# A hand-ordered transformer block on five engines: another order of all steps, with weight loads, a modulation product and weight splits moved

## The reference

```python
ada = silu(c) @ W_ada + b_ada                      # [32, 6*288]
shift_msa, scale_msa, gate_msa, shift_mlp, scale_mlp, gate_mlp = split(ada, 6)
h = layernorm(x) * (1 + scale_msa) + shift_msa
qkv = h @ W_qkv + b_qkv                            # 288 -> 864
attn = softmax(q k^T / sqrt(18))                   # 16 heads, 256 x 256
x = x + gate_msa * ((attn @ v) @ W_proj + b_proj)
h = layernorm(x) * (1 + scale_mlp) + shift_mlp
x = x + gate_mlp * (gelu(h @ W_fc1 + b_fc1) @ W_fc2 + b_fc2)   # 288 -> 1152 -> 288
```

## Time and profile before

| | |
|---|---|
| Time, median of 3 runs | 1203.75 us (1203.28 to 1208.13) |
| The profiled execution's own time | 1203.89 us |
| Its span, first to last instruction | 1202.1 us |
| Mean granted TensorE clock, share of full speed | 0.984 |
| PE busy | 1158.4 us (96%), 10375 matmuls |
| DVE busy | 920.6 us (77%) |
| ACT busy | 858.0 us (71%) |
| POOL busy | 579.2 us (48%) |
| HEAD of TensorE | first step at 14.8 us |

### The profile page before, as it was taken

The page is one execution under the profiler, slowest core; times in us unless marked ns, Lnnn a source line. Parts: engine busy times, 40 slices in busy tenths (PEclk is TensorE's granted clock), DMA queues, the critical chain, the costliest instruction groups (busy, mean ns, idle before and its releaser), DMA issues.

```text
span 1202.1 us, 28774 instructions
## 1 busy us (share of the span) xinstructions
PE 1158.4 (96%) x10375; PEld 993.9 (83%) x10375; DVE 920.6 (77%) x1928; ACT 858.0 (71%) x1485; POOL 579.2 (48%) x619
## 2 busy tenths in 40 slices
PE   6888999999999999999999999999999999999987
PEld 5666788888888888888888888888888888888777
DVE  5578878878878788887778888877888887877553
ACT  4378777777777777777777787777777777778721
POOL 3012444555544445554454555445455544544664
PEclk9779999999999999999999999999999999999999
DMA  9454554455555445555544555555445555444220
GB/s 276 137 172 156 163 164 147 150 175 168 164 159 163 149 148 173 166 171 164 163 151 151 159 179 165 165 159 167 143 149 181 164 165 161 158 148 156 83 68 20
DMA packets 133814, 186.93 MB, mean 156 GB/s; under 512 B 24284, under 2 KB 102150, under 8 KB 133675
## 3 DMA queue, kind: packets, MB, share of 16 engines
q1 hardware_dynamic: 133513, 184.66, 48.9%
q10 hardware_dynamic: 162, 0.44, 0.1%
HBM read 119.92 MB, written 64.60 MB: 153 GB/s over the span
## 4 chain that ended last, share of the span: by engine, by line
PE 92%; DVE 3%; ACT 2%; DMA 1%; issue 1%; SPq 0%; POOL 0%; ACTq 0%; POOLq 0%; DVEq 0%
PE a_bank L855 13%; PE x_bank L768 12%; PE turn_bank L822 10%; PE b_bank L855 9%; PE score_bank L793 7%; PE st_bank L810 7%; PE b_bank L869 7%; PE b_bank L870 6%; PE b_bank L871 6%; PE a_bank L836 5%; PE x_bank L776 5%; PE x_bank L742 2%; PE a_bank L742 1%; ACT e L942 1%; PE x_bank L745 1%
## 5 line engine op out<-in xcount | busy, mean ns | idle before, releaser
L1128 DVE TENSOR_REDUCE mx<-score_bank 128x2 f32<-128x512 f32 x512 | 332.3, 685 | 94.6 <-PE score_bank L793 92.8
L942 ACT ACTIVATE e<-st_bank 128x1024 f32<-128x1024 f32 x256 | 262.3, 1024 | 163.9 <-PE st_bank L810 163.3
L1285 POOL TENSOR_TENSOR gl<-gl_raw,gh 128x512 fp32r<-128x512 f32 (+1 forms) x160 | 197.2, 1241 | 180.8 <-DVE gh L1193 180.8
L935 ACT CAST ql<-mxt 4x256 fp32r<-4x256 f32 x512 | 205.7, 402 | 5.3
L869 PE MATMUL b_bank<-w,gh 128*128 128x288 f32 x576 | 179.1, 311 | 2.0 <-DVE tmp L1199 1.9
L870 PE MATMUL b_bank<-w,gh 128*128 128x288 f32 x576 | 170.6, 296 | 0.0
L871 PE MATMUL b_bank<-w,gl 128*128 128x288 f32 x576 | 169.6, 295 | 0.0
L822 PE MATMUL turn_bank<-e,ve 128*32 128x256 f32 x2048 | 125.8, 387 | 0.1
L810 PE MATMUL st_bank<-ql,kl 58*128 58x256 f32 x1024 | 117.9, 309 | 6.1 <-ACT e L942 5.0
L793 PE MATMUL score_bank<-kl,ql 58*128 58x256 f32 x1024 | 120.7, 314 | 2.7 <-DVE mx L1128 1.9
L855 PE MATMUL a_bank<-xh,w 128*128 128x256 f32 x640 | 112.2, 298 | 5.5 <-DVE xr L1107 4.0
(11 more groups left out here) (152 smaller groups left out, 2490.9 us busy)
## 6 DMA issues: line engine op xcount, KB each, us to landing
qk_rows<-qst SPq DMA_DIRECT2D x128, 256.0 KB, 3.7
ql<-qk_rows SPq DMA_DIRECT2D x384, 72.0 KB
kl<-qk_rows SPq DMA_DIRECT2D x378, 72.0 KB
o_rows<-on SPq DMA_DIRECT2D x128, 128.0 KB
gate<-gates SPq DMA_DIRECT2D x32, 432.0 KB, 4.5
xin<-in_x SPq DMA_DIRECT2D x32, 288.0 KB, 4.1
x<-in_x SPq DMA_DIRECT2D x32, 288.0 KB, 4.0
out<-x SPq DMA_DIRECT2D x32, 288.0 KB, 2.2
```

The lines of the kernel that those rows point to most:

```text
L935: last = nc.scalar.copy(rows[:, :, :, a, :], src)
L942: nc.scalar.activation(e[:, j % 4, :, :, :].rearrange("p i u l -> p (i u l)"), st_bank[:, :, :, :].rearrange("p i u l -> p (i u l)"), ACT. ...
L1128: nc.vector.tensor_reduce(mx[:, j // HP, i, :, col:col + 1], score_bank[i][:, :].rearrange("p (t l) -> p t l", t=NT), AX.X, ALU.max).then_ ...
L1285: nc.gpsimd.tensor_tensor(gl[:, cols], g[:, cols], gh[:, cols].bitcast(F32), ALU.subtract).then_inc(g_lo, 1)
```

## The change

All fifteen tables are replaced by others; the steps in them are the same, save for what follows.

- **TensorE's period.** In the old ORDER the 16 steps of 58 rows (`s`, `st`) stand as seven pairs and two single steps; one `pv` stands alone between `fc2` and `qk`, one behind a single `s`. In the new one they stand as eight pairs; one `pv` is behind a pair, one in front of a pair. Three pairs are followed by a turning (before: four), and one turning (`("xt", 2, 1)`) stands between `fc1` steps.
- **Scores by head.** For sequences 0 and 1 the step `s` is replaced by two steps `sh`, one for each head: 2 matmuls, both in the same half of the array.
- **Second modulation in pieces.** `mod` becomes ten steps of 3 products each, spread over the start of HEAD.
- **Weight loads.** Loads 7 to 11 leave the block ahead of SyncE's HEAD and become steps `load`, the first behind `("qkr", 0, 5)`.
- **Splits.** Of the nine weight splits in HEAD, the two of the packed 32 channels (5 and 8) stay on VectorE, the other seven (3, 4, 6, 7, 9, 10, 11) go to GpSimd, with a semaphore of their own, `w_late`.

The diff, with the other tables and the rest of the HEAD lists left out:

```diff
 PE_ORDER = [
-    ("fc2", -3, 0), ("proj", -2, 0), ("st", 0, 1), ("s", 0, 6), ("xt", 2, 0), ("proj", -2, 1), ("st", 0, 2),
-    ("s", 0, 7), ("xt", 2, 1), ("fc2", -3, 1), ("st", 0, 3), ("fc2", -3, 2), ("pv", 0, 0), ("qk", 2, 0),
-    ("fc2", -3, 3), ("s", 1, 0), ("st", 0, 4), ("lt", -2, 0), ("fc2", -3, 4), ("s", 1, 1), ("st", 0, 5),
-    ("lt", -2, 1), ("qk", 2, 1), ("fc2", -3, 5), ("s", 1, 2), ("st", 0, 6), ("fc1", -2, 0), ("s", 1, 3),
-    ("st", 0, 7), ("qk", 2, 2), ("fc1", -2, 1), ("s", 1, 4), ("pv", 0, 1), ("fc1", -2, 2), ("v", 2, 0),
-    ("fc1", -2, 3), ("st", 1, 0), ("s", 1, 5), ("fc1", -2, 4), ("v", 2, 1),
+    ("st", 0, 2), ("s", 0, 7), ("fc1", -3, 2), ("xt", 2, 1), ("fc1", -3, 3), ("fc1", -3, 4), ("qk", 2, 0),
+    ("fc2", -3, 0), ("proj", -2, 0), ("s", 1, 0), ("st", 0, 3), ("proj", -2, 1), ("fc2", -3, 1), ("qk", 2, 1),
+    ("s", 1, 1), ("st", 0, 4), ("pv", 0, 0), ("fc2", -3, 2), ("st", 0, 5), ("s", 1, 2), ("lt", -2, 0), ("qk", 2, 2),
+    ("fc2", -3, 3), ("st", 0, 6), ("s", 1, 3), ("lt", -2, 1), ("fc2", -3, 4), ("st", 0, 7), ("s", 1, 4), ("v", 2, 0),
+    ("fc2", -3, 5), ("pv", 0, 1), ("s", 1, 5), ("st", 1, 0), ("v", 2, 1), ("fc1", -2, 0), ("st", 1, 1), ("s", 1, 6),
+    ("xt", 3, 0), ("fc1", -2, 1),
 ]
...
 PE_HEAD = [
+    ("xt", 0, 0), ("xt", 0, 1), ("qk", 0, 0), ("qk", 0, 1), ("qk", 0, 2), ("gate2", 0, 0), ("gate5", 0, 0),
+    ("v", 0, 0), ("gate5", 0, 1), ("v", 0, 1), ("mod", 0, 0), ("gate5", 0, 2), ("xt", 1, 0), ("gate2", 0, 1),
+    ("mod", 0, 1), ("xt", 1, 1), ("mod", 0, 2), ("mod", 0, 3), ("sh", 0, 0), ("sh", 0, 1), ("gate2", 0, 2),
+    ("sh", 0, 2), ("sh", 0, 3), ("qk", 1, 0), ("sh", 0, 4), ("sh", 0, 5), ("mod", 0, 4), ("sh", 0, 6), ("sh", 0, 7),
+    ("qk", 1, 1), ("sh", 0, 8), ("sh", 0, 9), ("mod", 0, 5), ("mod", 0, 6), ("mod", 0, 7), ("mod", 0, 8),
+    ("mod", 0, 9), ("qk", 1, 2), ("sh", 0, 10), ("st", 0, 0), ("sh", 0, 11), ("v", 1, 0), ("sh", 0, 12),
+    ("st", 0, 1), ("sh", 0, 13), ("v", 1, 1), ("st", 0, 2), ("sh", 0, 14), ("xt", 2, 0), ("sh", 0, 15), ("st", 0, 3),
+    ("xt", 2, 1), ("pv", 0, 0), ("qk", 2, 0), ("sh", 1, 0), ("st", 0, 4), ("sh", 1, 1), ("sh", 1, 2), ("st", 0, 5),
...
 ACT_HEAD = [
+    ("xt", 0, 0), ("xt", 0, 1), ("round", 0, 0), ("round", 0, 1), ("qk", 0, 0), ("qk", 0, 1), ("qk", 0, 2),
+    ("v", 0, 0), ("qkr", 0, 0), ("round", 0, 2), ("qkr", 0, 1), ("qkr", 0, 2), ("v", 0, 1), ("qkr", 0, 3),
+    ("qkr", 0, 4), ("qkr", 0, 5), ("xt", 1, 0), ("xt", 1, 1), ("round", 0, 3), ("round", 0, 4), ("qk", 1, 0),
+    ("round", 0, 5), ("qk", 1, 1), ("mb", 0, 0), ("qk", 1, 2), ("st", 0, 0), ("v", 1, 0), ("st", 0, 1), ("v", 1, 1),
+    ("st", 0, 2), ("xt", 2, 0), ("st", 0, 3), ("xt", 2, 1), ("mb", 0, 1), ("qk", 2, 0), ("st", 0, 4),
...
 DVE_HEAD = [
+    ("qk", 0, 1), ("qk", 0, 2), ("ln1_stats", 1, 0), ("ln1_apply", 1, 0), ("ln1_apply", 1, 1), ("xt", 1, 0),
+    ("ln1_stats", 2, 0), ("xt", 1, 1), ("max", 0, 0), ("max", 0, 1), ("split", 0, 5), ("gates", 0, 0),
+    ("ln1_apply", 2, 0), ("max", 0, 2), ("max", 0, 3), ("max", 0, 4), ("max", 0, 5), ("qk", 1, 0), ("max", 0, 6),
+    ("split", 0, 8), ("max", 0, 7), ("mt", 0, 0), ("qk", 1, 1), ("ln1_apply", 2, 1), ("max", 0, 8), ("mod", 0, 0),
+    ("max", 0, 9), ("max", 0, 10), ("qk", 1, 2), ("max", 0, 11), ("ln1_stats", 3, 0), ("max", 0, 12), ("max", 0, 13),
...
 POOL_HEAD = [
+    ("clr", 0, 0), ("ln1_stats", 0, 0), ("clr", 0, 1), ("xt", 0, 0), ("clr", 1, 0), ("split", 0, 3),
+    ("ln1_stats", 1, 0), ("split", 0, 4), ("ln1_stats", 2, 0), ("xt", 1, 0), ("split", 0, 6), ("clr", 1, 1),
+    ("split", 0, 7), ("clr", 2, 0), ("xt", 2, 0), ("ln1_stats", 3, 0), ("clr", 2, 1), ("xt", 3, 0),
+    ("ln1_stats", 4, 0), ("clr", 3, 0), ("clr", 3, 1), ("ol", 0, 0), ("xt", 4, 0), ("proj", 0, 0), ("proj", 0, 1),
...
 SYNC_HEAD = [
+    ("qkr", 0, 5), ("load", 0, 7), ("qkr", 0, 12), ("qkr", 0, 13), ("qkr", 0, 14), ("qkr", 0, 15), ("qkr", 0, 16),
+    ("load", 0, 8), ("qkr", 0, 17), ("qkr", 0, 18), ("qkr", 0, 19), ("qkr", 0, 20), ("ln1_stats", 3, 0),
+    ("qkr", 0, 21), ("load", 0, 9), ("qkr", 0, 22), ("qkr", 0, 23), ("qkw", 1, 0), ("load", 0, 10), ("qkw", 1, 1),
+    ("qkw", 1, 2), ("res", 0, 0), ("qkr", 1, 0), ("qkr", 1, 1), ("qkr", 1, 2), ("qkw", 1, 3), ("qkw", 1, 4),
+    ("qkr", 1, 3), ("qkr", 1, 4), ("qkr", 1, 5), ("qkr", 1, 6), ("qkr", 1, 7), ("qkr", 1, 8), ("qkr", 1, 9),
+    ("qkr", 1, 10), ("qkr", 1, 11), ("qkr", 1, 12), ("ln1_stats", 4, 0), ("qkr", 1, 13), ("qkr", 1, 14),
+    ("qkr", 1, 15), ("qkr", 1, 16), ("qkr", 1, 17), ("qkr", 1, 18), ("qkr", 1, 19), ("qkr", 1, 20), ("qkr", 1, 21),
...
         minus_set = sem("minus_set")
         minus_rows = sem("minus_rows")
         w_split = sem("w_split")
+        w_late = sem("w_late")
         c_loaded = sem("c_loaded")
         ada_first = sem("ada_first")
         choice = sem("choice")
@@ -467,7 +471,7 @@
                            for v in (w2_raw[:, 1, f:f + 3, :], w2[:, 0, f:f + 3, :], w2[:, 1, f:f + 3, :]))
             loads.append(("fc2", w_fc2, None, raw, hi, lo, 3 * C, f))
         I_PROJ = 5
-        N_FIRST = 3
+        N_FIRST, N_EARLY = 3, 7
         w_loaded = sems("w_loaded", len(loads))
 
 
@@ -684,9 +688,9 @@
             sp.wait_ge(minus_set, 1)
             for r0, nr in ((O_REM[2][0], O_REM[2][2]), (O_REM[3][0], O_REM[3][2] + 1)):
                 sp.dma_start(minus_p[r0:r0 + nr, 0:1], minus_p[r0:r0 + nr, 1:2]).then_inc(minus_rows, 16)
-            for i in range(N_FIRST, len(loads)):
+            for i in range(N_FIRST, N_EARLY):
                 load_weights(i)
-            run(SYNC_HEAD, SYNC_ORDER, SYNC_TAIL, {"ln1_stats": ln1_stats, "res": res, "qkw": qkw, "qkr": qkr, "ow": ow,
+            run(SYNC_HEAD, SYNC_ORDER, SYNC_TAIL, {"load": lambda _b, i: load_weights(i), "ln1_stats": ln1_stats, "res": res, "qkw": qkw, "qkr": qkr, "ow": ow,
                              "sr": sum_read, "sw": rc_write, "rr": rc_read, "or": o_read, "store": store})
             for i in range(2):
                 sp.wait_ge(stored[i], 16 * (B // 2))
@@ -702,23 +706,31 @@
             last.then_inc(ada_turned, 1)
 
             pe.wait_ge(ada_sT, 1)
+            def mod_piece(n, i, c, r):
+
+                c0 = MOD_OF[2 * n + i] * C
+                cols = slice(c0 + c * P, min(c0 + (c + 1) * P, c0 + C))
+                for k, (_r, nr) in enumerate(K_ROWS):
+                    rows = nr + (k == 2)
+                    to = mod_of[n][:, i, c, :] if c < 2 else mod_of[n][REM * r:REM * (r + 1), i, c, :]
+                    last = nc.tensor.matmul(to, w_ada_sb[k][0:rows, cols], sT[0:rows, k, :],
+                                            start=(k == 0), stop=(k == 2))
+                return last
+
+            MOD_PIECES = [(i, c, r) for i in range(2) for c in range(3) for r in range(1 if c < 2 else 3)]
+
             def mod_columns(n):
 
-                for i in range(2):
-                    c0 = MOD_OF[2 * n + i] * C
-                    for c in range(3):
-                        for k, (_r, nr) in enumerate(K_ROWS):
-                            rows = nr + (k == 2)
-                            for r in range(1 if c < 2 else 3):
-                                to = mod_of[n][:, i, c, :] if c < 2 else mod_of[n][REM * r:REM * (r + 1), i, c, :]
-                                cols = slice(c0 + c * P, min(c0 + (c + 1) * P, c0 + C))
-                                last = nc.tensor.matmul(to, w_ada_sb[k][0:rows, cols], sT[0:rows, k, :],
-                                                        start=(k == 0), stop=(k == 2))
+                for i, c, r in MOD_PIECES:
+                    last = mod_piece(n, i, c, r)
                 last.then_inc(ada_mod, 1)
 
-            def second_mod(_b, _n):
-                pe.wait_ge(ada_rest, 16 * 3)
-                mod_columns(1)
+            def second_mod(_b, n):
+                if n == 0:
+                    pe.wait_ge(ada_rest, 16 * 3)
+                last = mod_piece(1, *MOD_PIECES[n])
+                if n == len(MOD_PIECES) - 1:
+                    last.then_inc(ada_mod, 1)
 
             def gate_rows(v, k):
                 if k == 0:
@@ -796,6 +808,23 @@
                         if t == NT - 1:
                             last.then_inc(s_full[i], 1)
 
+            def s_head(b, h):
+                j, i = h // 2, h % 2
+                slot, use = half_use(b, j // HP)
+                if j % HP == 0:
+                    pe.wait_ge(qk_rows[slot], 16 * READS * (use + 1))
+                if b == 0 and h == 0:
+                    pe.wait_ge(consts, FIRST_SET)
+                    pe.wait_ge(kl_chosen, SLOTS)
+                    pe.wait_ge(ql_cleared, 1)
+                wait(pe, s_max[i], PAIRS * b + j)
+                rows = slice(TILE * i, TILE * i + KM)
+                for t in range(NT):
+                    last = nc.tensor.matmul(score_bank[i][:, t * L:(t + 1) * L],
+                                            ql[rows, slot, j % HP, t * P:(t + 1) * P], kl[rows, slot, j % HP, :],
```

(25 more changed lines are left out.)

136 lines of the change are left out of this document (60 added, 76 removed), and 148 rows, old and new, of tables (ACT_HEAD, ACT_ORDER, ACT_TAIL, DVE_TAIL).

## The result

The change makes the kernel slower: 1258.32 us (median of 4 runs, 1256.40 to 1260.13) against 1203.93, ratio 1.0442 [1.0417, 1.0468]. The forecast was 1184, the range 1175 to 1198. By span, 1258.0 against 1202.1 us, the loss of 55.9 us is made up as follows. TensorE's steps were matched one by one between the two traces, and a length is read from the first matmul of a step to the first of another.

What follows compares the result with a forecast made beforehand. TensorE, never idle between about 140 and 1085 us, was taken to bound the kernel. 1203.9 less 14.6 for the periods and 5 for the first `st`, the rest at 0, gave 1184 us, range 1175 to 1198.

Steps and rivals of the forecast that it cites:

- The edges of TensorE's period: Repeated order: pairing score steps and two fewer groups between products save 0.54 us a period, 14.6 us over 27 periods.
- Whether the others keep up: Repeated order: no new wait, with slacks of 0.2 us at `st` 5's exponential and 0.4 at the casts before `st` (1,0).
- The rule that was weighed: Splits in HEAD: GpSimd shares its way to SBUF with VectorE, so up to 14.6 us of DVE work could stretch, once.
- The rival of the other side: Repeated order: DVE late with a half's last maxima behind a POOL-stretched subtraction, 1.0 us wait a period, 1211 us; chance 0.07.
- First `st` at -5: Start: late loads and the second modulation in pieces bring the first `st` 5 us earlier, bounds 0 and 9.
- the prediction's signs of being wrong: PE idle before `st_bank` every period, longer `pv`, `W_fc1` casts on ACT released by a DMA, half clock past 110 us.
- Rest of HEAD at 0: HEAD: splits moved to POOL's idle time and `sh` steps in half the array together count 0, range -4 to +4.
- The tail at 0: End of the run: same order in its last sixty steps, so 0 us, range -2 to +2.
- Two readings that enter no term: HEAD: clock below full from 35 to 70 us and in three more slices; 3.6 us of moved splits behind first `st`.

Runs made afterwards that it cites:

- without contention: Changed kernel with GpSimd's subtractions for xt, ol and fc1 cut to 4 or 8 columns a block, low parts left out of sums: 1211.81 us, ratio 1.0063.
- 3: Kernel before with one part alone, weight loads 7 to 11 behind the first row reads: 1208.00 us, ratio 1.0016.
- 9: Second of the two repairs, with the first modulation's loops in the order of the kernel before: 1224.03 us, ratio 1.0179.
- 4: First of the two repairs: 1236.61 us, ratio 1.0254; the same with all twelve weight loads issued ahead of the row reads: 1240.30 us, ratio 1.0287.
- 6: Seven weight splits on GpSimd in the kernel before: 1213.34 us; all splits back on VectorE in the changed kernel: 1256.06; in the second repair: 1231.52.
- 8: Last six pieces of the second modulation moved ahead of the first score product, in the changed kernel: 1257.21 us; in the second repair: 1229.22.
- two repairs: Changed kernel, VectorE's xt(2,1), max(0,15) before fc1(-3,1), ln1_stats(3,0) later: 1236.61 us; second, also GpSimd's ol behind fc1(-2,1) and further VectorE moves: 1227.79.

## Why the prediction was wrong

- **The edges of TensorE's period: right.** Forecast 34.3 us without waits, from 0.35, 0.33 and 0.10 an edge; 34.43 was measured without contention, 34.29 of it without the one wait left. So the term of -14.6 us was right for TensorE's own work. The 27 periods came out 35.0 us longer, not 14.6 shorter.
- **"Whether the others keep up": the step that failed.** It put new waits at nothing, and 1.95 us a period were measured. It looked at the two places where the score steps came closest to their exponential and their casts. Both held: no idle in front of `st_bank` or `pv` in any period. The place that failed was not on the list: `("qk", 2, 0)` behind `("xt", 2, 1)`. In the old order the last stretched gelu rounding ends at 528.2 and the first cast of the next normalization begins at 535.3; the new lists bring the roundings, the normalization and POOL's output subtraction together in 6 us, and there DVE runs at POOL's pace. The slacks were worked out with DVE and POOL at the durations that each had in the old order (0.42 for this subtraction, against 1.39), as if these were properties of the operation.
- **The rule that was weighed, and put in the wrong place.** The sharing of ways to SBUF was set against the splits in the start alone ("could stretch, once"). The row that it took from the Trainium skill (GPSIMD Engine Reference, Specifications) names DVE instructions in a 2-port perf mode beside those with two SBUF inputs; the prediction kept only the second kind, and three of the four stretched operations are casts, with one input. Groups of the kernel before, of the same 70 us, would have told: the two of `xn` above, 1293 against 410 ns, and the gelu cast, where half a cast takes 283 ns and a whole one 680, which is not the pace of one operation.

```profile
L1193 DVE CAST gh<-gl_raw 128x512 fp32r<-128x512 f32 x8 | 5.3, 680 | 0.4 <-ACT gl_raw L980 0.4
...
L1193 DVE CAST gh<-gl_raw 128x256 fp32r<-128x256 f32 x2 | 0.6, 283 | 0.0
```

- **The rival of the other side** named the mechanism (a subtraction of POOL that stretches DVE), the wrong victim (the last maxima; they read PSUM and aren't stretched) and a price of 1.0 us a period; it was 1.95. Its chance of 0.07 was too low for a change that rewrites all lists of four engines against each other.
- **First `st` at -5: wrong, +3.9 measured** (62.2 against 58.3). The row writes landed in 3.3 us (7.1 in the earlier trace rows), as forecast; the scores then waited 3.74 us for the row reads, and late loads alone didn't help before either (3). The issues of the first 50 us, PE's first score product, and ACT's rounding of load 7, after:

```profile
qk_rows<-qst SPq DMA_DIRECT2D x4, 256.0 KB, 3.3
```

```profile
41.94 0.80 PE L823 MATMUL score_bank<-kl,ql 58*128 58x256 f32 x4 [3.74 <-DMA kl<-qk_rows]
43.25 1.15 ACT L920 CAST w<-w_raw 128x1152 fp32r<-128x1152 f32 x1 [4.54 <-DMA w_raw<-in_L_cond_W_fc]
```

  The first turning was 2.05 late for the loops (9), which "pieces" had not suggested. The last line is one of the prediction's signs of being wrong: late weights do hold ACT, but ACT's next work, the cast of `("qk", 1, 0)`, then waits 3.90 for PE, so this isn't what decided.
- **Rest of HEAD at 0: wrong.** From the first `st` to the repeated order the changed kernel loses another 9.6 us. Two parts were priced in the kernel before: splits on POOL +7 in the median, late loads +2.5 (their interval reaches 0). But they don't add in the new order, and taken back one by one (4, 6, 8) the parts move the start by 4 us at most and the median by nothing that can be told. With every engine's list of HEAD unchanged the start lay at 158.7, 150.5 and 153.4 (the change, its two repairs), and half clock before it at 61, 41 and 50 us. So of the 13.5 us 2 are shown at the first turning (loops). The others can't be told from what one profiled execution and another differ by, half clock included; without contention the start was 153.5, no earlier than in the repairs. What holds the rest stays open.
- **The tail at 0: wrong,** +7.3, of which 3.5 is work handed over from HEAD and 3.8 is lost.
- **Two readings that enter no term were off.** The row of PE clock has two slices below full, from 30 to 90 us, and not three beside the stretch from 35 to 70. And the splits that left DVE behind the first `st` are load 7 and loads 9 to 11, 3744 columns and 4.4 us, not 3.6.

## What to carry to other kernels

Before VectorE and GpSimd are re-ordered against each other, lay their lists side by side and mark every SBUF-to-SBUF cast or two-input operation that would start inside a GpSimd operation: as the four here, it ends when that one has ended, and can meet the next. What bounds the distance then is the number of such operations ahead of the one that TensorE wants, not their busy time. And in an order without slack a move that saves a tenth of a microsecond is judged by the two or three waits that it newly exposes: bank drained, exponential done, remainder ready.

## What the hardware showed

- A stretched DVE operation depends on what runs beside it: 0.43 us for a 128x512 cast alone, 1.14 to 1.47 beside subtractions of 1.3 to 1.5; 0.68 to 0.69 us for a maximum out of PSUM either way.
- Three groups of 32 columns of TensorE's array work at the same time if their products alternate: 0.62 against 1.78 us for 18 products, both at full clock.
- 34 idle-filling products kept full clock from 31.9 to 36.3 us and halved the following half-clock stretch (13.6 to 6.8 us), but another came at 53.3 to 70.4 where before had one at 55.8 to 72.8: before the repeated order half clock fell from 34.1 to 30.7 us only. The filler moves the fall of the clock more than it removes it.
